# Two halves of a state read-out, each with its own wait, in a hand-ordered RWKV and FP4 kernel

## The reference

```
def step(state, inp):
    rt, kt, vt, wt = inp
    kv = kt[..., :, None] * vt[..., None, :]
    out = jnp.einsum('bhk,bhkv->bhv', rt, state + u[None, :, :, None] * kv)
    return (state * wt[..., None] + kv, out)
```

## Time and profile before

| what | value |
|---|---|
| median of 3 runs | 2931.07 us |
| the profiled execution | 2933.48 us |
| its span, first to last instruction | 2931.7 us |
| PE busy | 2725.0 us, 93% |
| DVE busy | 2349.0 us, 80% |
| ACT busy | 1389.7 us, 47% |
| POOL busy | 1279.2 us, 44% |
| mean granted TensorE clock | 0.974 |

### The profile page before, as it was taken

How to read it: one execution, slowest core, us unless ns; L and a number is a source line. 1 busy time by engine, 2 the same in 40 slices (tenths; PEclk the granted TensorE clock), 3 DMA queues, 4 the chain that set the end, 5 groups by cost and what they waited for, 6 DMA issues and landing times.

```text
span 2931.7 us, 82824 instructions
## 1 busy us (share of the span) xinstructions
PE 2725.0 (93%) x34621; PEld 2171.8 (74%) x34621; DVE 2349.0 (80%) x5345; ACT 1389.7 (47%) x2899; POOL 1279.2 (44%) x1457
## 2 busy tenths in 40 slices
PE   5679999999999999999999999999999999999874
PEld 3567777777777777777777777777777777777653
DVE  5667888888888888888888888888888888888763
ACT  2344455554545555454555545455554445555320
POOL 3344444445444444544444444444444444444310
PEclk7789999999999999999999999999999999999987
DMA  4000000000000000000000000000000000000000
GB/s 153 14 5 9 13 9 9 9 12 13 13 13 9 9 9 13 13 13 13 9 9 9 12 13 13 13 13 5 9 13 12 13 13 13 7 7 13 9 8 7
DMA packets 36849, 41.77 MB, mean 14 GB/s; under 512 B 3272, under 2 KB 35200, under 8 KB 36480
## 3 DMA queue, kind: packets, MB, share of 16 engines
q1 hardware_dynamic: 35696, 36.32, 3.9%
q10 hardware_dynamic: 784, 0.16, 0.1%
HBM read 28.08 MB, written 8.39 MB: 12 GB/s over the span
## 4 chain that ended last, share of the span: by engine, by line
PE 74%; ACT 13%; DVE 7%; issue 4%; POOL 1%; ACTq 0%; DMA 0%; DVEq 0%; POOLq 0%
PE ps_all L1530 12%; PE ps_all L1317 11%; PE ps_all L1516 10%; PE ps_all L1549 8%; PE ps_all L1325 8%; PE ps_all L1567 5%; PE ps_all L1428 3%; PE ps_all L1355 3%; ACT L898 3%; PE ps_all L1309 2%; PE ps_all L1341 2%; ACT tok L898 2%; PE ps_all L1423 2%; PE ps_all L1486 2%; PE ps_all L1497 1%
## 5 line engine op out<-in xcount | busy, mean ns | idle before, releaser
L771 POOL TENSOR_TENSOR mixin<-mixin,hT_tm 128x512 f32<-128x512 f32 x320 | 398.0, 1260 | 384.9 <-DVE mixin L1118 384.1
L1516 PE MATMUL ps_all<-chan,cwk 128*128 128x256 f32 x1536 | 374.0, 391 | 6.2 <-DVE chan L1097 5.5
L1530 PE MATMUL ps_all<-cwv,chan 128*128 128x256 f32 x1536 | 348.4, 383 | 0.6 <-DVE S L1194 0.6
L1516 PEld LDWEIGHTS ps_all<-chan,cwk 128*128 128x128 f32 x1536 | 288.6, 193 | 58.2 <-issue 17.2
L1530 PEld LDWEIGHTS ps_all<-cwv,chan 128*128 128x128 f32 x1536 | 286.7, 190 | 49.6 <-issue 10.3
L1118 DVE SCALAR_TENSOR_TENSOR mixin<-ps_all,vcol,sxrk 128x256 f32<-128x256 f32 x640 | 271.5, 473 | 29.9 <-PE ps_all L1355 19.8
L912 ACT ACTIVATE chan<-ps_all 128x512 f32<-128x512 f32 x192 | 114.9, 598 | 265.9 <-PE ps_all L1516 265.9
L751 POOL TENSOR_TENSOR rstd<-var,powc 128x2 f32<-128x2 f32 x224 | 178.2, 796 | 123.6 <-DVE var L1057 120.2
L1168 DVE COPY_PREDICATED att<-masks,ps_all 128x256 f32<-128x256 uint8 x384 | 203.3, 530 | 11.5 <-DVE att L1168 0.5
L1549 PE MATMUL ps_all<-gateT,ffn_work 128*128 128x352 f32 x512 | 184.1, 483 | 5.0 <-ACT ffn_work L871 2.6
L795 POOL TENSOR_TENSOR grstd<-gvar,powc 128x8 f32<-128x8 f32 x64 | 115.6, 1807 | 150.2 <-DVE gvar L1201 150.2
(11 more groups left out here) (191 smaller groups left out, 6620.3 us busy)
## 6 DMA issues: line engine op xcount, KB each, us to landing
xin<-in_L_attn_x_dram SPq DMA_DIRECT2D x32, 256.0 KB, 2.8
tok<-in_L_attn_x_dram SPq DMA_DIRECT2D x32, 256.0 KB, 2.7
out_dram<-x SPq DMA_DIRECT2D x32, 256.0 KB, 3.0
cwk<-in_L_attn_cWk_dram SPq DMA_DIRECT2D x2, 768.0 KB, 8.1
cwv<-in_L_attn_cWv_dram SPq DMA_DIRECT2D x2, 768.0 KB, 10.2
ffn_work<-in_L_wmod_dram SPq DMA_DIRECT2D x2, 512.0 KB, 5.1
tok<-in_L_ffn_w_down_dram SPq DMA_DIRECT2D x1, 704.0 KB, 4.2
tok<-in_L_ffn_w_gate_dram SPq DMA_DIRECT2D x1, 640.0 KB, 8.6
```

The costliest lines, as they stand in the source:

```text
L771: pool.tensor_tensor(m, m, hT["tm", l][:, :, :, 1:P + 1].rearrange("p k c t -> p (k c) t"), ALU.add).then_inc(ev["mixed"][b], 1)
L1516: ins = pe.matmul(bank(b, "ck", lj, "k")[:, m * TT:(m + 1) * TT], cwk[:, l, k, n:n + P], k_in[:, k, :], start=(k == 0), stop=(k == KC - 1))
L1530: ins = pe.matmul(bank(b, "cv", l, "v")[:, c * D:(c + 1) * D], relu[t // 2][:, t % 2, c * P:(c + 1) * P], cwv[:, l, t, :], start=(t == 0), ...
```

## The change

`ov` is split by token half. Half 1 goes first and waits only for the mid state (`emptied ... "s"`). The wait for `t` (`filled ... "t"`, the last result of stage `so`, on PE itself) moves between the halves, with a second `pe_passed` increment. The order inside changes with it: where four matmuls in a row fell on four quarters, now eight in a row alternate between the two quarters of half 1, and then eight between the two of half 0. Number, shape and operands of the matmuls stay the same.

```diff
             def ov(i, b, l):
 
                 emptied(pe, i, b, "so", l, "s")
-                filled(pe, i, b, "so", l, "t")
                 pe.sem_inc(pe_passed, 1)
-                for c in range(NC):
-                    for k in range(KC):
-                        for e, x in TILES:
-                            q = (e + x) % 2
-                            p, t, n = slice(e * HS, (e + 1) * HS), c * P + q * HH, (c * KC + k) * HS
-                            ins = pe.matmul(bank(b, "so", l, "o", e)[swapped(e, q), n:n + HS], r_last[b][p, k, t:t + HH], S[b][p, q, k, c, :],
-                                            start=False, stop=(c == NC - 1 and k == KC - 1), skip_group_check=True)
+                for q in (1, 0):
+                    if not q:
+                        filled(pe, i, b, "so", l, "t")
+                        pe.sem_inc(pe_passed, 1)
+                    for c in range(NC):
+                        for k in range(KC):
+                            for e in range(HP):
+                                p, t, n = slice(e * HS, (e + 1) * HS), c * P + q * HH, (c * KC + k) * HS
+                                ins = pe.matmul(bank(b, "so", l, "o", e)[swapped(e, q), n:n + HS], r_last[b][p, k, t:t + HH], S[b][p, q, k, c, :],
+                                                start=False, stop=(c == NC - 1 and k == KC - 1), skip_group_check=True)
                 ins.then_inc(full_of(b, "so", l, "o"), 1)
```

## The result

The changed kernel took 2949.3 us (median of 6 runs, 2945.69 to 2950.98), the kernel before 2931.1 (6 runs, 2927.8 to 2933.31). The ratio is 1.0061, 95% interval 1.005 to 1.0072: +18.2 us, where +3.0 was forecast and the range ended at 2944.0. The profiled execution took 2947.98 us, its span is 2946.2, 14.5 more than before.

A forecast was written before the change was run, and what follows sets the result against it. PE's own list was taken to bound the kernel. 32 x 0.10 for chain 0 plus 32 x 0 for chain 1, less 0.2 for early tiles, gave +3.0 us: 2934.1 us forecast, range 2930 to 2944.

The forecast's parts named there:

- What bounds the kernel, and the wait that is moved: PE's list sets the time; before chain 0's `ov` the mid state ends last, so removing `t`'s wait gains at most 0.02.
- x = 0.16, the cost 0.10: Chain 0's `ov`: half 0 starts x behind half 1, 0.05 for handing on eight matmuls plus 0.11 for the wait instruction.
- x is about 0.02 ... Cost: 0: Chain 1's `ov`: the sequencer runs ahead, both waits pass before `ov` begins, so half 0 follows half 1 at about 0.02.
- `mf` misled me: Stage behind chain 1's `ov`: its 16 passes in 1.17 us were read as quarters overlapping across runs of two matmuls.
- 0.10 and not 0.35: Cost per chain 0 `ov`: 0.10 by the main forecast, 0.35 if half 0 waits for half 1's last pass.
- The slack of chain 1: `mf` behind chain 1's `ov` waits for ACT's tanh, so 0.04 or 0.05 us of delay costs nothing there.
- The price of the wait, 0.11: Between the halves of chain 0's `ov`: the satisfied wait instruction takes 0.11 us, unhidden because the pair behind is idle.
- Rival 2: Border of halves in every `ov`: half 0 waits for half 1's last pass; +20.9 us, 2952; chance 0.11.
- Rival 1: In `ov`, two matmuls of a quarter may wait, not more; x = 0.23 in chain 0, +9.4 us, 2940.5; chance 0.22.
- Rival 3: In `ov`, the second wait passes without a gap, x under 0.06 in both chains; nothing costs or gains, 2931; chance 0.14.
- rival 4: Stalls before `ov` fall into the pause between halves or shift to stages that hide them; faster, 2927; chance 0.06.

The follow-up runs named there:

- experiment 4: Kernel before, with both waits in front of `ov` and all four matmuls of one quarter in a row, then the next quarter's: 2982.19 us, ratio 1.0165.
- experiment 5: Kernel before, both waits in front; three matmuls per quarter for half 1, three for half 0, then the last of each: 2941.87 us, ratio 1.0026.
- experiment 1: Kernel before, with the change's order of quarters but both waits in front of `ov`, no second wait between the halves: 2948.06 us, ratio 1.005.
- experiment 3: Changed kernel with halves alternating, two matmuls per quarter at a time, wait for `t` behind the first four: 2938.64 us, ratio 1.0016 to the kernel before.
- experiment 9: Kernel before, with DVE's last mask copy ahead of a feed-forward product and half of chain 1's `lev.1` between chain 0's `so` and `ov`: 2943.36 us, ratio 1.0035.

## Why the prediction was wrong

- **What bounds the kernel, and the wait that is moved: right.** PE's list sets the time. `ov` starts 0.36 behind `so` as before, held by the mid state. As forecast, only where the mid state is early does half 1 start sooner, in 3 of chain 0's `ov`s of the profiled execution, such as this one (0.05 behind the last start of `so`, but with a longer group, so that `ck.2` comes 1.00 behind that start where it came 0.96 in such a tile before):

```profile
2373.64 0.22 PE L1454 MATMUL ps_all<-tok 64*64 64x64 f32 x1
2373.69 1.02 PE L1488 MATMUL ps_all<-S,mixin 64*64 64x64 f32 x32
```

- **The step that failed: "x = 0.16, the cost 0.10" in chain 0, and "x is about 0.02 ... Cost: 0" in chain 1.** x is 0.294 in both. The place was right, the border of the halves; what delays half 0 was not. I took the sequencer's lead for a queue at the quarters. The earlier trace rows shows a wait instruction passing PE's sequencer while half of the 16 matmuls had not started. That the sequencer is ahead does not say that a later matmul may overtake a waiting one on its way to an idle quarter. The changed kernel and experiments 4 and 5 fit one limit: one running and one waiting per quarter, and the line stands at the third. So four in a row cost 0.28, wherever the wait instruction is; chain 1, for which I had reckoned nothing because there is time ahead of it, pays the same, less the slack before `mf`.
- **`mf` misled me.** Two matmuls of a quarter in a row are exactly what the limit lets through the earlier trace rows. It showed that quarters overlap across runs of two and nothing about runs of four. For those I took the lower of my two figures, 0.10 and not 0.35, though the trace had shown neither.
- **The slack of chain 1: right.** 0.04 or 0.05 were forecast to be swallowed before `mf`; the last start moved by 0.281 and `mf` by 0.24.
- **The price of the wait, 0.11: about right in size, wrong in place.** In the changed kernel it costs nothing: half 0 begins at 0.294 with it and, in experiment 1, without it. It appears, at 0.13, where only four matmuls stand ahead of it and PE had been idle (experiment 3, chain 0).
- **The rivals.** Rival 2, the pairs one behind the other, to which I gave a chance of 0.11, said +20.9 us and is the nearest in time. Its mechanism is not what happens: half 0 does not wait for half 1's last pass (reckoned at 0.41, seen at 0.463) but for its third matmuls (0.29), and by its rule experiment 4 would have cost +88 us, not +49. Rival 1 had the right kind of limit with the wrong number, two waiting instead of one. Rival 3, no cost, is out by the groups' length, and rival 4, a gain from lost stalls, by the 8.8 and 9.1 us above.

The Trainium skill's sentence in "TensorE: Matmul & The Clock Gate", "What overlaps and what doesn't", that matmuls start strictly in program order, pointed to rival 2, whose time was nearer than mine. Taken literally it disagrees with these runs: half 0 starts at 0.294, ahead of half 1's fourth matmuls (0.398 and 0.405 in chain 1), and experiment 4's group takes 1.51 us and not the 2.1 reckoned by that rule.

## What to carry to other kernels

When small matmuls share the array, the order in which they fall on its parts can be worth more than a wait moved by some hundredths. In fp32 matmuls of 64x64, as here, rotating the parts with every matmul was fastest, and more than two for one part in a row held up the others. Before a wait is split or moved, read on its releaser's end whether it binds at all, and whether the edit changes the rotation on the way. And a step that waits for all its banks at its start is bound by the last of them; each wait belongs in front of its own first use.

## What the runs showed of the hardware

- All runs fit a quarter of the array that takes one running and one waiting fp32 matmul, while a third one for it holds up whatever is behind. With two quarters in alternation, three matmuls for each before the others cost 0.165 us and four 0.281 per `ov` of 16; each quarter's four in a row cost 0.81 to 0.84 (starts over 1.29 and 1.32 instead of 0.477).
- A quarter that starts needs 0.107 us from its first to its second pass (0.078 for the first quarter alone where PE had stood idle), then 0.058 per pass of 64 columns.
- A satisfied wait between matmuls costs nothing when eight matmuls stand ahead of it (1.0008, 0.9999 to 1.0016) and 0.13 us when PE had been idle and four stand ahead (half 0 at 0.154 instead of 0.026, experiment 3).
- The record of PE's wait instruction is 51 ns long when the wait is satisfied, and 749 ns in experiment 9, where it ends 0.05 behind the product that releases it; the timeline calls that time "issue".
